# Attention in a two-layer transformer kernel: scores issued a head at a time, the product with the values in one block

## The chip, the cores and the metric

The kernel runs on one core of a Trainium2 chip. Its time is the device time of one execution in microseconds (us). TensorE, VectorE (DVE), ScalarE (ACT), GpSimd (POOL) and the DMA queue of SyncE (SP) each work through a list of instructions of their own, in order, and wait for each other by semaphores.

## The reference

Two layers over 2048 tokens of width 256, each `x + ga * attention(LN(x))` and then `x + gb * ffn(LN(x))`; shifts, scales and gates come from a small product. Attention has 16 heads of width 16. Cut to what matters here:

```python
# layer 0: causal, with a penalty that grows with the distance
S = jnp.einsum('hid,hjd->hij', K, Q) * HEAD_DIM ** -0.5
S = jnp.where(delta < 0, -jnp.inf, S) + decay          # decay = -(i - j)
C = jax.nn.softmax(S, axis=-1)
attn = jnp.einsum('hij,hjd->hid', C, V)
# layer 1: every token sees every token
scores = jnp.einsum('bhqd,bhkd->bhqk', q, k) * EMBED_DIM ** -0.5
probs = jax.nn.softmax(scores, axis=-1)
attn = jnp.einsum('bhqk,bhkd->bhqd', probs, v)
```

The softmax needs each row's maximum; the kernel computes the scores once to find the maxima and a second time, with the maximum already subtracted, for the exponentials.

## The kernel before

**Units and steps.** Attention goes by units: a unit is 512 rows (a chunk, of 4) times a group of four heads (of 4), 16 units a layer. A unit goes through its keys in steps of 128 keys: 16 steps a unit in layer 1, and 4, 8, 12 or 16 in layer 0 for chunks 0 to 3 (`steps_of`). So layer 0 has 160 steps and layer 1 has 256. In layer 0 the last four steps of each unit are diagonal: they leave out the first 0, 128, 256 or 384 rows (`off`) and add a triangle of -1e30 by two more products per head (line 690).

**One step.** For each of four heads: a score product (line 682), 128 keys by 512 rows, written to one of three PSUM banks (0, 1 and 2, in turn, over all steps); ScalarE's exponential (line 875) from that bank into `probs`, which has two buffers by step; and the product with the values (line 707) from `probs` into bank 7, where the unit's steps accumulate. The product with the values of step s is issued during step s + 1. A head's scores use 52 partitions that begin at 0 (even heads) or at 64 (odd heads). The four heads' values have 17 columns each and write to partitions 0, 32, 64 and 96 of bank 7; each float32 product is run as two instructions in the trace.

**Work beside the steps.** The maxima of a later unit are computed in pairs of heads: two score products (line 654, in layer 0 with the mask of line 660) into the two banks of a slot, and a reduction of 128 x 1024 by VectorE (line 1075). A reduction for each 128 rows, head pair and 512 keys makes 32 a unit in layer 1. There are two slots (banks 3 and 4, 5 and 6); nearly all other TensorE work that isn't a step (transposes, projections) takes a slot in turn too, and waits until the slot's work before last has been drained (`open_slot`). When all maxima of a unit are there, VectorE forms two parts of each (lines 1083 to 1088), TensorE transposes them (`mt`, line 667), ScalarE copies them and SP's DMAs place them among the rows (`place`). At a unit's end ScalarE copies bank 7 (`oc`, line 890), and TensorE transposes the sums (`ft`, line 717); after four units follow `bt`, `op`, `st`, `nm` and `ln`, the output projection and the next normalisation.

**What sets the order.** `attention_walk` writes one list by hand; every engine walks the same list and picks its own entries. For each step: the scores of heads 0 and 1 (`sc` with 0), the first half of the step's maxima, the first 256 columns of the last step's product with the values (`pv` with 0), the scores of heads 2 and 3 (`sc` with 1), the rest of the maxima, the other 256 columns (`pv` with 1), and then the transposes that fall to this step. At a unit's first step the whole 512 columns are in `pv` 0. Most steps have two pairs of maxima.

**Semaphores.** `s_e` counts completed scores, `s_p` exponentials, `s_pv` steps whose product is complete, `s_oc` copies of bank 7. A score e waits for exponential e - 3, the last user of its bank (counted from the kernel's first score); the product waits for all four exponentials of its step; a step's first exponential waits for the product of two steps before.

Of the kernel before, what the change touches and what calls it, by code (L numbers as in the profile page):

```python
# [10 lines left out]
ACT = mybir.ActivationFunctionType  # L11
AX = mybir.AxisListType

P = 128
# [4 lines left out]
CH = 512  # L19
# [64 lines left out]
def attention_walk(y, done):  # L84
# [15 lines left out]
    for n in range(NU):  # L100
        steps = steps_of(y, n)
        for k in range(steps):
# [5 lines left out]
            out += work[:half]  # L108
            if s:
                out.append(("pv", y, s - 1, m, j, 0))  # L110
            out.append(("sc", y, s, n, k, 1))
            out += work[half:]
            if s:
                out.append(("pv", y, s - 1, m, j, 1))
# [20 lines left out]
    out += [("pv", y, total - 1, NU - 1, steps_of(y, NU - 1) - 1, z) for z in range(2)] + [("oc", y, NU - 1)]  # L135
# [105 lines left out]
def adaln_two_layers(nc, a):  # L241
    ctx = ExitStack()
    with ctx:
# [343 lines left out]
        def _(pe):  # L587
# [83 lines left out]
            def scores(y, s, n, jt, hp):  # L671
                i, g = n // NG, n % NG
                if jt == 0 and hp == 0:
                    pe.wait_ge(s_mrow, 64 * (y * NU + n + 1))
                off = max(0, jt - TPC * i) * P if CAUSAL[y] else 0
                diag = CAUSAL[y] and jt >= TPC * i
                e = HG * (S0[y] + s) + 2 * hp
                for par in range(2):
                    if e + par >= 3:
                        pe.wait_ge(s_p, e + par - 2)  # L680
                    at = slice(64 * par, 64 * par + KS)
                    mm = pe.matmul(bank((e + par) % 3)[:, off:CH], keys[at, g * HP + hp, jt * P:(jt + 1) * P],  # L682
                                   rows[at, g, hp, off:CH], start=True, stop=not diag)
                    if not diag:
                        mm.then_inc(s_e, 1)
                if diag:
                    for z in range(2):
                        for par in range(2):
                            at = slice(64 * par, 64 * par + 64)
                            mm = pe.matmul(bank((e + par) % 3)[:, off:off + P], eye2[at, z, :], neg_e[at, z, :],  # L690
                                           start=False, stop=(z == 1))
                            if z == 1:
                                mm.then_inc(s_e, 1)

            def values(y, s, n, jt, z):
                i, g = n // NG, n % NG
                off = max(0, jt - TPC * i) * P if CAUSAL[y] else 0
                lo, hi = (max(off, z * CH // 2), (z + 1) * CH // 2) if jt else (0, CH * (1 - z))
                if z == 0:
                    pe.wait_ge(s_p, HG * (S0[y] + s + 1))  # L700
                if jt == 0 and z == 0:
# [3 lines left out]
                if lo < hi:  # L705
                    for h in range(HG):
                        mm = pe.matmul(psum[32 * h:32 * h + VW, 7, lo:hi], v_sb[:, jt, g * HG + h, :],  # L707
                                       probs[:, (S0[y] + s) % 2, h, lo:hi], start=(jt == 0),
                                       stop=(z == 1 and jt == steps_of(y, n) - 1))
                    if z == 1 or jt == 0:  # L710
                        mm.then_inc(s_pv, 1)
# [123 lines left out]
        def _(act):  # L835
# [29 lines left out]
            def exps(y, s, n, jt, hp):  # L865
                i = n // NG
                off = max(0, jt - TPC * i) * P if CAUSAL[y] else 0
                if s == 0 and y == 0 and hp == 0:
                    act.wait_ge(s_mod, NLAY)
                if S0[y] + s >= 2 and hp == 0:  # L870
                    act.wait_ge(s_pv, S0[y] + s - 1)
                for par in range(2):
                    e = HG * (S0[y] + s) + 2 * hp + par
                    act.wait_ge(s_e, e + 1)
# [371 lines left out]
```

## Time and profile before

| | |
|---|---|
| median of 3 runs | 1858.12 us (1856.98 to 1858.46) |
| profiled execution | 1858.49 us, span 1856.7 us |
| TensorE matmul, busy | 1653.7 us (89%), 12812 instructions |
| TensorE weight load, busy | 704.9 us (38%) |
| VectorE, busy | 1161.5 us (63%) |
| ScalarE, busy | 1005.3 us (54%) |
| GpSimd, busy | 61.4 us (3%) |
| maximum reductions, line 1075 | 832, 912.1 us |
| exponentials, line 875 | 1664, 845.7 us |
| product with the values, line 707 | 6144 instructions, 495.8 us |
| scores, line 682 | 1664, 352.0 us |

The profile is of one execution. Layer 0's attention runs from about 100 to 553 us, layer 1's from about 838 to 1485; the feed-forward stages lie between and behind them. Matmuls are pipelined, so a matmul's busy time (some 0.38 us for 512 columns) is longer than its distance to the next one; the distance from start to start is what adds up. In the windows below, each engine has its busy time and in brackets its count of instructions. In the rows in order of time, neighbouring instructions of one line are merged (x8), and the bracket at the end gives the idle time before the first and what released it.

### The profile page before, as it was taken

To read this page: it belongs to the slowest core of one execution; us is meant where nothing else is said; L and a number is where in the kernel's file an instruction comes from. 1 tells how busy PE (TensorE), PEld (TensorE's weight loads), DVE (VectorE), ACT (ScalarE), POOL (GpSimd) and SP (SyncE) were. 2 spreads that over 40 slices of the span, in tenths; PEclk is the share of its full clock that TensorE was granted. 3 is DMA by queue.
4 is the path that set the end of the run, shared out by engine and by line. 5 is a ranking of instruction groups with operands and counts; after the bars stand their busy time and mean duration, and the time that the engine had idled before them with its cause. 6 is when DMAs were issued, how large, how long until landed. Compare 5 with 4: busy or idle time off the path is not lost.

```text
span 1856.7 us, 32528 instructions
## 1 busy us (share of the span) xinstructions
PE 1653.7 (89%) x12812; PEld 704.9 (38%) x12812; DVE 1161.5 (63%) x1430; ACT 1005.3 (54%) x1913; POOL 61.4 (3%) x96
## 2 busy tenths in 40 slices
PE   7888989889999987758998999899999988999998
PEld 4533333333335543412333333333332243645545
DVE  4477887988802334494998999899899033121221
ACT  1145667768881111008997899789888913121110
POOL 1200000010000000300000000000000020000000
PEclk9879999999999999758999999999999989999999
DMA  7610000000000210110200000000000010000000
GB/s 204 137 53 11 12 9 6 11 6 2 2 1 29 58 40 20 41 19 5 84 6 6 6 6 10 2 11 6 6 2 2 1 40 0 10 3 12 1 12 12
DMA packets 39542, 41.87 MB, mean 23 GB/s; under 512 B 7172, under 2 KB 37828, under 8 KB 39388
## 3 DMA queue, kind: packets, MB, share of 16 engines
q1 hardware_dynamic: 39396, 39.79, 8.2%
q8 instruction: 108, 1.77, 0.4%
q14 instruction: 38, 0.31, 0.1%
HBM read 29.02 MB, written 10.49 MB: 21 GB/s over the span
## 4 chain that ended last, share of the span: by engine, by line
PE 32%; DVE 24%; ACT 3%; issue 2%; DVEq 0%; ACTq 0%
DVE mpart L1075 20%; PE psum L748 6%; PE psum L773 6%; PE psum L707 6%; PE psum L752 6%; PE psum L682 3%; ACT probs L875 3%; PE psum L654 2%; PE psum L627 1%; DVE probs L1103 1%; DVE key_region L1106 1%; PE psum L736 1%; PE psum L783 1%; PE psum L639 0%; DVE attn_region L1023 0%
## 5 line engine op out<-in xcount | busy, mean ns | idle before, releaser
L1075 DVE TENSOR_REDUCE mpart<-psum 128x2 f32<-128x1024 f32 (+2 forms) x832 | 912.1, 1158 | 103.8 <-PE psum L654 84.2
L875 ACT ACTIVATE probs<-psum 128x512 f32<-128x512 f32 (+3 forms) x1664 | 845.7, 573 | 188.1 <-PE psum L682 107.5
L707 PE MATMUL psum<-probs,v_region 128*17 128x256 f32 (+2 forms) x6144 | 495.8, 395 | 14.6 <-ACT out_sb L890 7.9
L654 PE MATMUL psum<-key_region,row_region 50*128 50x512 f16 (+3 forms) x1664 | 327.1, 385 | 94.3 <-DVE mpart L1075 79.8
L682 PE MATMUL psum<-row_region,key_region 52*128 52x512 f16 (+3 forms) x1664 | 352.0, 380 | 11.6 <-ACT probs L875 10.3
L682 PEld LDWEIGHTS psum<-row_region,key_region 52*128 52x128 f16 x1664 | 97.2, 93 | 367.3 <-ACT probs L875 286.5
L748 PE MATMUL psum<-hT,ffn_w 128*128 128x512 f32 (+1 forms) x320 | 162.2, 631 | 41.9 <-DVE key_region L1106 20.6
L707 PEld LDWEIGHTS psum<-probs,v_region 128*17 128x17 f32 x6144 | 102.8, 95 | 206.7 <-issue 101.5
L654 PEld LDWEIGHTS psum<-key_region,row_region 50*128 50x128 f16 x1664 | 94.7, 94 | 191.7 <-DVE mpart L1075 137.4
L752 PE MATMUL psum<-hT,ffn_w 128*128 128x512 f32 (+1 forms) x320 | 152.7, 600 | 0.0
L914 ACT ACTIVATE probs<-psum 128x512 f32<-128x512 f32 (+1 forms) x56 | 33.4, 597 | 199.4 <-PE psum L748 199.4
L1066 DVE TENSOR_TENSOR x_sb<-psum,x_sb 128x1024 f32<-128x1024 f32 x16 | 19.6, 1224 | 162.9 <-PE psum L773 137.4
L1103 DVE TENSOR_TENSOR probs<-psum,probs 128x512 f32<-128x512 f32 x44 | 30.4, 692 | 130.4 <-PE psum L752 130.4
L748 PEld LDWEIGHTS psum<-hT,ffn_w 128*128 128x128 f32 (+1 forms) x320 | 57.6, 192 | 114.1 <-issue 56.6
L773 PE MATMUL psum<-v_region,key_region 128*128 128x256 f32 x448 | 97.5, 379 | 1.7 <-DVE key_region L1106 1.7
L752 PEld LDWEIGHTS psum<-hT,ffn_w 128*128 128x128 f32 (+1 forms) x320 | 61.1, 191 | 81.3 <-issue 81.3
L773 PEld LDWEIGHTS psum<-v_region,key_region 128*128 128x128 f32 x448 | 85.0, 190 | 15.4 <-issue 3.9
L914 ACT ACTIVATE probs<-psum,gate_s 128x512 f32<-128x512 f32 (+1 forms) x24 | 16.5, 686 | 121.7 <-PE psum L748 121.7
L1099 DVE SCALAR_TENSOR_TENSOR key_region<-psum,up_s,probs 128x512 f32<-128x512 f32 (+1 forms) x24 | 18.0, 749 | 92.6 <-PE psum L752 68.4
L851 ACT ACTIVATE hT<-psum,modc 128x512 f32<-128x512 f32 x32 | 23.1, 775 | 79.4 <-PE psum L616 79.4
L924 ACT ACTIVATE probs<-psum 128x1024 f32<-128x1024 f32 (+1 forms) x24 | 22.8, 952 | 61.3 <-PE psum L761 61.3
L1109 DVE TENSOR_TENSOR key_region<-psum,probs 128x512 f32<-128x512 f32 (+1 forms) x12 | 8.3, 689 | 70.9 <-PE psum L752 70.9
(101 smaller groups left out, 920.6 us busy)
## 6 DMA issues: line engine op xcount, KB each, us to landing
parts<-key_region SPq DMA_DIRECT2D x32, 256.0 KB, 2.5
key_region<-parts SPq DMA_DIRECT2D x48, 128.0 KB, 4.4
row_region<-parts SPq DMA_DIRECT2D x192, 32.0 KB
key_region<-in_wmod SPq DMA_DIRECT2D x2, 1536.0 KB, 12.2
x_sb<-in_x SPq DMA_DIRECT2D x4, 512.0 KB, 8.4
row_region<-mrow_t SPq DMA_DIRECT2D x128, 2.0 KB
out<-x_sb SPq DMA_DIRECT2D x16, 128.0 KB, 1.8
ffn_w<-in_w_gate SPq DMA_DIRECT2D x1, 1760.0 KB, 8.4
```

The lines of the kernel that those rows point to most:

```text
L654: mm = pe.matmul(bank(b + par)[:, 0:w], rows[at, g, hp, r * P:(r + 1) * P], keys[at, g * HP + hp, q * CH:q * CH + w], start=True, stop=not ...
L682: mm = pe.matmul(bank((e + par) % 3)[:, off:CH], keys[at, g * HP + hp, jt * P:(jt + 1) * P], rows[at, g, hp, off:CH], start=True, stop=not ...
L707: mm = pe.matmul(psum[32 * h:32 * h + VW, 7, lo:hi], v_sb[:, jt, g * HG + h, :], probs[:, (S0[y] + s) % 2, h, lo:hi], start=(jt == 0), sto ...
L748: mm = pe.matmul(psum[0:f, b, :], up_gate[y][0][:, d, c * P:c * P + f], hT[:, d, tok], start=(d == 0), stop=(d == KD - 1))
L752: mm = pe.matmul(psum[0:f, b + 1, :], up_gate[y][1][:, d, c * P:c * P + f], hT[:, d, tok], start=(d == 0), stop=(d == KD - 1))
L773: mm = pe.matmul(both(b)[:, r * D:(r + 1) * D], hid[y][tc % 2][0:f, c, r * P:(r + 1) * P], down[y][0:f, c, :], start=(c == 0), stop=(c == ...
L851: ins = nc.scalar.activation(hT[:, c, tc * CH:(tc + 1) * CH], bank(b + c), ACT.Identity, bias=modc[:, y, i:i + 1], scale=modc[:, y, i + 2: ...
L875: nc.scalar.activation(probs[:, (S0[y] + s) % 2, 2 * hp + par, off:CH], psum[:, e % 3, off:CH], ACT.Exp, scale=SCALES[y]).then_inc(s_p, 1)
L914: nc.scalar.activation(sil[k % 2][0:f, :], psum[0:f, bank_of(item), :], ACT.Silu, scale=gate_s[0:f, c:c + 1] if y == 0 else 1.0).then_inc( ...
L924: nc.scalar.activation(wx[k % 2][:, 0:n, :], psum[:, bank_of(item):bank_of(item) + n, :], ACT.Identity).then_inc(drained(*item)[0], 1)
L1075: V.tensor_reduce(mpart[:, n % NG, at:at + 2, q:q + 1], psum[:, b:b + 2, 0:w], AX.X, ALU.max).then_inc(drained(*item)[0], 1)
L1103: V.tensor_tensor(utmp[k % 2], up, sil[k % 2], ALU.mult).then_inc(s_ut, 1)
```

## The change

`attention_walk` now issues, for each step: the score of head 0, the first half of the maxima, the scores of heads 1 and 2, the rest of the maxima, the score of head 3, and then the last step's product with the values over all its columns at once. `scores` and `exps` handle one head a call instead of two; in the diagonal steps a head's mask products follow its own score. `values` issues four products (eight instructions in the trace) of up to 512 columns instead of twice that many of 256. Banks, buffers and what each semaphore counts stay.

```diff
--- before.py
+++ after.py
@@ -106,12 +106,11 @@
             m, j = (n, k - 1) if k else (n - 1, steps_of(y, n - 1) - 1 if n else 0)
             out.append(("sc", y, s, n, k, 0))
             out += work[:half]
+            out += [("sc", y, s, n, k, h) for h in (1, 2)]
+            out += work[half:]
+            out.append(("sc", y, s, n, k, 3))
             if s:
-                out.append(("pv", y, s - 1, m, j, 0))
-            out.append(("sc", y, s, n, k, 1))
-            out += work[half:]
-            if s:
-                out.append(("pv", y, s - 1, m, j, 1))
+                out.append(("pv", y, s - 1, m, j))
             if s and k == 0:
                 out.append(("oc", y, n - 1))
             if k == 0 and n and n + 3 < NU:
@@ -132,7 +131,7 @@
                     out.append(("nm", 2 * y + 1, i))
                 if k == 6:
                     out.append(("ln", 2 * y + 1, i))
-    out += [("pv", y, total - 1, NU - 1, steps_of(y, NU - 1) - 1, z) for z in range(2)] + [("oc", y, NU - 1)]
+    out += [("pv", y, total - 1, NU - 1, steps_of(y, NU - 1) - 1), ("oc", y, NU - 1)]
     return out
 
 
@@ -668,47 +667,36 @@
                                    identh[:, :], start=True, stop=True)
                 mm.then_inc(filled(*item)[0], 1)
 
-            def scores(y, s, n, jt, hp):
+            def scores(y, s, n, jt, h):
                 i, g = n // NG, n % NG
-                if jt == 0 and hp == 0:
+                if jt == 0 and h == 0:
                     pe.wait_ge(s_mrow, 64 * (y * NU + n + 1))
                 off = max(0, jt - TPC * i) * P if CAUSAL[y] else 0
                 diag = CAUSAL[y] and jt >= TPC * i
-                e = HG * (S0[y] + s) + 2 * hp
-                for par in range(2):
-                    if e + par >= 3:
-                        pe.wait_ge(s_p, e + par - 2)
-                    at = slice(64 * par, 64 * par + KS)
-                    mm = pe.matmul(bank((e + par) % 3)[:, off:CH], keys[at, g * HP + hp, jt * P:(jt + 1) * P],
-                                   rows[at, g, hp, off:CH], start=True, stop=not diag)
-                    if not diag:
-                        mm.then_inc(s_e, 1)
+                e = HG * (S0[y] + s) + h
+                if e >= 3:
+                    pe.wait_ge(s_p, e - 2)
+                at = slice(64 * (h % 2), 64 * (h % 2) + KS)
+                mm = pe.matmul(bank(e % 3)[:, off:CH], keys[at, g * HP + h // 2, jt * P:(jt + 1) * P],
+                               rows[at, g, h // 2, off:CH], start=True, stop=not diag)
                 if diag:
+                    at = slice(64 * (h % 2), 64 * (h % 2) + 64)
                     for z in range(2):
-                        for par in range(2):
-                            at = slice(64 * par, 64 * par + 64)
-                            mm = pe.matmul(bank((e + par) % 3)[:, off:off + P], eye2[at, z, :], neg_e[at, z, :],
-                                           start=False, stop=(z == 1))
-                            if z == 1:
-                                mm.then_inc(s_e, 1)
-
-            def values(y, s, n, jt, z):
+                        mm = pe.matmul(bank(e % 3)[:, off:off + P], eye2[at, z, :], neg_e[at, z, :], start=False, stop=(z == 1))
+                mm.then_inc(s_e, 1)
+
+            def values(y, s, n, jt):
                 i, g = n // NG, n % NG
-                off = max(0, jt - TPC * i) * P if CAUSAL[y] else 0
-                lo, hi = (max(off, z * CH // 2), (z + 1) * CH // 2) if jt else (0, CH * (1 - z))
-                if z == 0:
-                    pe.wait_ge(s_p, HG * (S0[y] + s + 1))
-                if jt == 0 and z == 0:
+                pe.wait_ge(s_p, HG * (S0[y] + s + 1))
+                if jt == 0:
                     pe.wait_ge(*drained("v", y, (NCH - 1) if not CAUSAL[y] else i))
                     if y * NU + n:
                         pe.wait_ge(s_oc, y * NU + n)
-                if lo < hi:
-                    for h in range(HG):
-                        mm = pe.matmul(psum[32 * h:32 * h + VW, 7, lo:hi], v_sb[:, jt, g * HG + h, :],
-                                       probs[:, (S0[y] + s) % 2, h, lo:hi], start=(jt == 0),
-                                       stop=(z == 1 and jt == steps_of(y, n) - 1))
-                    if z == 1 or jt == 0:
-                        mm.then_inc(s_pv, 1)
+                off = max(0, jt - TPC * i) * P if CAUSAL[y] else 0
+                for h in range(HG):
+                    mm = pe.matmul(psum[32 * h:32 * h + VW, 7, off:CH], v_sb[:, jt, g * HG + h, :],
+                                   probs[:, (S0[y] + s) % 2, h, off:CH], start=(jt == 0), stop=(jt == steps_of(y, n) - 1))
+                mm.then_inc(s_pv, 1)
 
             def sums_transpose(item):
                 b = open_slot(item)
@@ -862,18 +850,17 @@
                     nc.scalar.activation(stage[(k - 1) % 2][:, f, 0, :], bank(bank_of(item) + f), ACT.Identity,
                                          bias=(b_row, b_col)[side][:, f:f + 1]).then_inc(s_h, 1)
 
-            def exps(y, s, n, jt, hp):
+            def exps(y, s, n, jt, h):
                 i = n // NG
                 off = max(0, jt - TPC * i) * P if CAUSAL[y] else 0
-                if s == 0 and y == 0 and hp == 0:
+                if s == 0 and y == 0 and h == 0:
                     act.wait_ge(s_mod, NLAY)
-                if S0[y] + s >= 2 and hp == 0:
+                if S0[y] + s >= 2 and h == 0:
                     act.wait_ge(s_pv, S0[y] + s - 1)
-                for par in range(2):
-                    e = HG * (S0[y] + s) + 2 * hp + par
-                    act.wait_ge(s_e, e + 1)
-                    nc.scalar.activation(probs[:, (S0[y] + s) % 2, 2 * hp + par, off:CH], psum[:, e % 3, off:CH],
-                                         ACT.Exp, scale=SCALES[y]).then_inc(s_p, 1)
+                e = HG * (S0[y] + s) + h
+                act.wait_ge(s_e, e + 1)
+                nc.scalar.activation(probs[:, (S0[y] + s) % 2, h, off:CH], psum[:, e % 3, off:CH],
+                                     ACT.Exp, scale=SCALES[y]).then_inc(s_p, 1)
 
             def copy_maximum(item):
                 act.wait_ge(*filled(*item))
```

## Rows read from the trace of the kernel before

**Rows 1.** Windows: layer 1 and its end; busy (count) of PE, PEld, DVE, ACT, POOL; clock, DMA

```profile
870.00:1440.00 570.00, 536.28 (x5410) 177.63 (x5402) 531.63 (x548) 490.30 (x924) 3.79 (x6) 0.99 0.04 12
1440.00:1485.00 45.00, 42.38 (x412) 11.65 (x409) 0.68 (x2) 43.50 (x85) 0.00 (x0) 1.00 0.01 1
```

**Rows 2.** Chain of waits, layer 1: start, length, engine, tile, line, count

```profile
1086.37 15.94 DVE mpart L1075 x14
...
1108.09 13.68 DVE mpart L1075 x12
1125.30 15.94 DVE mpart L1075 x14
```

**Rows 3.** Order in time (start, length), TensorE, a plain step

```profile
921.40 0.39 PE L682 MATMUL psum<-row_region,key_region 52*128 52x512 f16 x2
921.63 0.38 PE L654 MATMUL psum<-key_region,row_region 50*128 50x512 f16 x2
921.94 0.63 PE L707 MATMUL psum<-probs,v_region 128*17 128x256 f32 x8
922.50 0.42 PE L682 MATMUL psum<-row_region,key_region 52*128 52x512 f16 x2
...
923.63 0.39 PE L682 MATMUL psum<-row_region,key_region 52*128 52x512 f16 x2
```

**Rows 4.** Order in time, TensorE, a step without maxima

```profile
1446.47 0.58 PE L682 MATMUL psum<-row_region,key_region 52*128 52x512 f16 x2
1447.15 0.63 PE L707 MATMUL psum<-probs,v_region 128*17 128x256 f32 x8
1447.71 0.39 PE L682 MATMUL psum<-row_region,key_region 52*128 52x512 f16 x2
```

**Rows 5.** Order in time, TensorE, a unit's second step

```profile
955.53 1.05 PE L707 MATMUL psum<-probs,v_region 128*17 128x512 f32 x8 [0.40 <-ACT out_sb L890]
956.52 0.39 PE L682 MATMUL psum<-row_region,key_region 52*128 52x512 f16 x2
...
957.64 0.39 PE L682 MATMUL psum<-row_region,key_region 52*128 52x512 f16 x2
958.45 0.39 PE L654 MATMUL psum<-key_region,row_region 50*128 50x512 f16 x2 [0.42 <-DVE mpart L1075]
```

**Rows 6.** Order in time, lone scores, two places

```profile
1019.65 1.08 ACT L875 ACTIVATE probs<-psum 128x512 f32<-128x512 f32 x2
...
1020.30 0.39 PE L682 MATMUL psum<-row_region,key_region 52*128 52x512 f16 x1 [0.69 <-ACT probs L875]
...
1020.51 0.40 PE L654 MATMUL psum<-key_region,row_region 50*128 50x512 f16 x2
...
1441.44 0.09 PEld L682 LDWEIGHTS psum<-row_region,key_region 52*128 52x128 f16 x1 [0.33 <-ACT probs L875]
...
1441.76 0.41 PE L707 MATMUL psum<-probs,v_region 128*17 128x256 f32 x4
```

**Rows 7.** Order in time, from a score to its exponential

```profile
942.20 0.39 PE L682 MATMUL psum<-row_region,key_region 52*128 52x512 f16 x2
...
942.62 1.75 ACT L875 ACTIVATE probs<-psum 128x512 f32<-128x512 f32 x3 [0.42 <-PE psum L682]
...
1006.84 0.39 PE L682 MATMUL psum<-row_region,key_region 52*128 52x512 f16 x2
...
1007.32 1.63 ACT L875 ACTIVATE probs<-psum 128x512 f32<-128x512 f32 x3 [3.81 <-PE psum L682]
```

**Rows 8.** Order in time, TensorE, behind the transposed maxima

```profile
940.52 0.39 PE L682 MATMUL psum<-row_region,key_region 52*128 52x512 f16 x2
...
941.32 0.39 PE L654 MATMUL psum<-key_region,row_region 50*128 50x512 f16 x2 [0.41 <-DVE mpart L1075]
```

**Rows 9.** Order in time, TensorE, a diagonal step

```profile
472.02 0.30 PE L690 MATMUL psum<-neg_e,eye 64*128 64x128 bf16 x4
472.13 0.40 PE L654 MATMUL psum<-key_region,row_region 50*128 50x512 f16 x2
```

## The prediction

> **What bounds the kernel now.** Two attention stages, 160 steps in the causal layer 0 and 256 in layer 1, take more than half of the time. I read the windows by stretch first [rows 1]. From 870 to 1440 us TensorE, VectorE and ScalarE are all 86 to 94% busy, so no share tells which one sets the pace; the reader is to see only that TensorE's clock is full (0.99) and that the last 45 us have hardly any VectorE work and ScalarE busy for 43.5. Then the chain of waits: in layer 1 its long pieces are maximum reductions, a unit of 16 steps begins again every 38.93 us (1125.30 - 1086.37), and from x14 against x12 one reduction costs (15.94 - 13.68) / 2 = 1.13 us [rows 2]. Two reductions a step are 2.26 us, 32 a unit 36.2 us. Then the order in time of a plain step [rows 3]: pair of scores, pair of maxima (+0.23), half of the product with the values (+0.31), next pair of scores (+0.56), and the same again: 921.40 to 923.63 is 2.23 us. VectorE falls behind by 0.03 a step and is caught up where the walk puts transposes. So the stage is tied: VectorE 2.26, TensorE's own instructions 2 x (0.23 + 0.31 + 0.56) = 2.2, ScalarE four exponentials. In steps without maxima the pace is 2.12 us [rows 4], and there the circle is visible: second score pair at 1446.47, its exponentials, values at 1447.15 (+0.68), next scores at 1447.71 (+0.56).
>
> **The change, part by part.** Nothing is computed differently; SP's and POOL's lists keep their order, and the transfers' waits count the same completed scores. Three things change on TensorE.
>
> *Half as many instructions with the values.* Two times (0.31 + 0.56) per step becomes one block of eight 512-column instructions. Such a block exists at each unit's first step: 955.53 to the next score 956.52, 0.99 us [rows 5]. Entry stays as it is after a lone score, 0.32 (1441.44 to 1441.76) [rows 6]. So 1.74 becomes 1.31 and the gain is 0.43 minus what follows.
>
> *Pairs of scores broken.* Heads of a pair lie in partitions 0 and 64 and both stream in the same 0.23 us [rows 3]. Now head 0 stands alone before a maximum, heads 1 and 2 pair up, head 3 stands alone: three slots of 0.23 for scores where there were two. A lone score is followed by the next maxima after 0.21 (1020.30 to 1020.51) [rows 6], so it does cost a slot and hides nothing. TensorE's own time per step is then 4 x 0.23 (head 0, maxima, heads 1 and 2, maxima) + 0.32 (head 3) + 0.99 = 2.23 against 2.2 before: nothing gained or lost. Bounds of a lone score: 0 (if the next maximum could stream beside it) and 0.23; I take 0.21 to 0.23, since the row shows it, and it will turn out not to matter, for the next term is longer.
>
> The Trainium skill (TensorEngine Tiling (Array Packing), Key Properties) says that changing the tiling mode drains TensorE. Scores take half the rows and the values' product a quarter of the columns, so the change halves the changes of mode, and the rows agree that they cost: 0.32 into the product against 0.23 between scores and maxima, and 0.13 lost per block (2 x 0.56 - 0.99). By that rule alone the step gets shorter by 0.2 us; its page TensorE: Matmul & The Clock Gate (Part 3) says that it is matmuls in distinct row groups that run at once, which takes the same 0.2 back for the broken pair. Were the rule on modes alone at work, the time would be that of rival 1.
>
> *A new wait, and this one decides.* Scores rotate through three banks: score e waits for exponential e - 3. For head 3 that is head 0 of the same step. Before, head 3 came 1.1 us after head 0 and the half product stood between two such circles; now head 3 is directly ahead of the whole product in TensorE's queue, and behind it wait the product, the next head 0 and the next maxima. The circle is head 0 -> exponential -> head 3 -> product -> next head 0. Its terms: score to exponential 0.48 with ScalarE idle (1006.84 to 1007.32; for the second half's first exponential it is 0.42, 942.20 to 942.62, so head 0 pays 0.06 more) [rows 7]; from the exponential's start to the score that waited for its bank 1020.30 - 1019.65 = 0.65 [rows 6]. So head 3 starts 0.48 + 0.65 = 1.13 after head 0, though its turn comes at 4 x 0.23 = 0.92. Then 0.32 and 0.99. Sum 1.13 + 0.32 + 0.99 = **2.44 us a step**, whether or not there are maxima. The same terms give today's 2.12: second score pair, 0.42, one exponential ahead in ScalarE's queue 0.49 (at most 43.5 us / 85 = 0.51), 0.65, together 1.56, + 0.56 = 2.12 [rows 1, 4, 6, 7]. ScalarE (4 x 0.5) and VectorE (2.26) both fit in 2.44, so they idle; a second maximum waits for its slot until 0.70, within 0.02 of its turn, and head 3's wait covers it.
>
> *The steps that are long today get shorter,* since VectorE no longer lags. In a regular unit of layer 1 38.93 - 16 x 2.23 = 3.25 us lie over the plain pace. Today the copy of the sums leaves TensorE idle for 0.40 ahead of the product, the transpose of the sums adds 0.56 (956.52 to 957.64 is 1.12, a half step's 0.56 without it), and the maximum behind it waits 0.58 for a slot (957.64 to 958.45 where 0.23 is usual) [rows 5]; the rest is around the transposed maxima, where I take 0.33 for the transpose itself, four products that fill one bank and stream in about a score's 0.23 with its turn-round, and a slot wait follows (940.52 to 941.32, 0.80 for 0.23) [rows 8]. After: the copy of the sums is out of TensorE's way but ahead of head 0's exponential, +0.12; the sums' transpose +0.6; its slot wait under head 3's; transposed maxima +0.33 and their slot wait +0.1 and +0.34 (VectorE has two reductions and the three small operations on the maxima, for which I take 0.8, still queued). Sum 1.5. So a regular unit changes by 16 x 0.21 - (3.25 - 1.5) = 3.3 - 1.75 = +1.6 us.
>
> **The sum.** Layer 1, units 1 to 13: 13 x 1.6 = +21 (three contain the output projection, whose stretch is VectorE's chain and absorbs a little; unit 1 has spare time before and loses more; they cancel). Units 0, 14 and 15: 32 steps without maxima x (2.44 - 2.12) = +10, and few plain ones: +11. Layer 0: by the walk 22 steps have no maxima, 14 of them full, 14 x 0.32 = 4.5; of the 82 other full ones I take half at the plain pace, 41 x 0.21 = 8.5 (the rest, with three or four maxima or beside transposes, wait for VectorE); its 64 diagonal steps lose the packing of the mask products too (the masks of two heads take 0.11 a half step, 472.02 to 472.13 [rows 9]; now each head has its own, some 0.2 to 0.4 more in the first two of four, less in the last two whose products are short), and many of them wait for three or four reductions a step anyway: +3. Together +16. Total 21 + 11 + 16 = +48. The profiled execution took 1858.5 (span 1856.7, 1.8 around it), 0.4 above the median of the runs, 1858.1; 1858.1 + 48 = **1906 us**.
>
> **The rivals.**
> 1. *VectorE stays the bound, faster* (7%). If head 0's exponential were done by 0.92 the circle would be TensorE's own 2.23 and the step VectorE's 2.26; a unit would be 36.2 + about 1.9 for the two other jobs of VectorE = 38.1, -0.8 x 14 = -11, steps without maxima +0.11 x 40 = +4: 1851. It decides from a way from head 0 to head 3 below 0.97 (2.26 + 0.02 - 0.32 - 0.99); the rows say 1.13. For it: today's plain step waits on TensorE for little, and half the mode changes go.
> 2. *The long waits hide it, slower by less* (17%). If stretches of layer 0 and the boundaries of units are VectorE's or POOL's chains more than I think, only layer 1's plain steps pay: about 130 x 0.21 less the boundary gain, and the steps without maxima: +20 to +30, 1883.
> 3. *The two streams beat against each other* (11%). Product, next head 0 and next maximum now come in one lump: 1.77 us without a new maximum (0.23 + 0.32 + 0.99 + 0.23). Where VectorE has one narrow causal reduction queued it starves, and after each transpose a late maximum delays head 3, then the whole product. At 0.3 more for each of the 64 diagonal steps and a unit's boundary: +15 to +20, 1924.
> 4. *No change* (4%): rivals 1 and the lone scores cancel.
> My forecast, 1890 to 1918, has 61%. The range 1876 to 1926 reaches into rivals 2 and 3 and leaves out rival 1 and their ends. About 0.2% (3.7 us) is what a measurement of this kernel can tell from no change: faster 0.07, same 0.04, slower 0.89.
>
> **What would show it.** Right: plain steps of layer 1 at 2.44 us, with and without maxima alike; head 3 alone, 1.13 after head 0, its weight load ended by ScalarE's exponential; VectorE waiting for TensorE some 0.15 a step instead of the reverse; eight 512-column instructions taking 0.99 to the next score; a unit at 40.5. Wrong: head 3 at 0.92 and steps at 2.26 (rival 1); steps at 2.44 but units still at 39 (rival 2); layer 0 losing more than 25 us (rival 3). The forecast falls if the exponential of a lone head 0 begins sooner than 0.48 or if a block of eight leaves sooner than 0.99 when it accumulates, for the block that I read is a unit's first.

## The result and the profile after

The change makes the kernel slower. The median of four runs is 1929.1 us (1914.0 to 1942.3) against 1857.9 us (1857.0 to 1858.5) for the kernel before: a ratio of 1.038, 95% interval 1.030 to 1.046. The direction was forecast; the size was not: 1906 was predicted, and 1929 lies 3 us above the upper end of the range. The profiled execution took 1942.3 us with a span of 1940.5; it is the slowest of the four, 13 us above their median. The four runs spread over 28 us, those of the kernel before over 1.5; nine later runs of the kernel before, though, went from 1855.6 to 1866.2.

The page, its rows of busy time and of TensorE's clock in 40 slices of 48.5 us (tenths of full speed):

```profile
PE 1719.5 (89%) x9996; PEld 663.8 (34%) x9996; DVE 1176.9 (61%) x1430; ACT 993.1 (51%) x1913; POOL 63.7 (3%) x96
PEclk9888989989959998755999999999999989999999
```

ScalarE's and VectorE's work is what it was (busy within 1.4%), and TensorE has 2,816 instructions fewer, which is the halved product with the values. In the clock the reader is to see the lone 5 in the twelfth slice (534 to 582 us). Of the groups, the product with the values and the weight loads of the scores:

```profile
L697 PE MATMUL psum<-probs,v_region 128*17 128x512 f32 (+3 forms) x3328 | 444.9, 609 | 0.1
L680 PEld LDWEIGHTS psum<-row_region,key_region 52*128 52x128 f16 x1664 | 127.6, 96 | 496.4 <-ACT probs L862 421.9
```

The weight loads of the scores (line 680) now sit 422 us behind ScalarE's exponentials, where it was 287 in the kernel before. A plain step of layer 1, TensorE's instructions in order of time, the place that answers to [rows 3]:

```profile
985.88 0.39 PE L680 MATMUL psum<-row_region,key_region 52*128 52x512 f16 x1
985.89 0.60 PE L653 MATMUL psum<-key_region,row_region 50*128 50x512 f16 x2
986.12 0.59 PE L680 MATMUL psum<-row_region,key_region 52*128 52x512 f16 x2
986.51 0.41 PE L653 MATMUL psum<-key_region,row_region 50*128 50x512 f16 x2
987.02 0.39 PE L680 MATMUL psum<-row_region,key_region 52*128 52x512 f16 x1
987.34 1.05 PE L697 MATMUL psum<-probs,v_region 128*17 128x512 f32 x8
988.32 0.39 PE L680 MATMUL psum<-row_region,key_region 52*128 52x512 f16 x1
```

Head 3 comes 1.14 after head 0 (987.02 - 985.88), the product 0.32 later, the next head 0 0.98 later: 2.44 us, the circle of the prediction term by term. The same line of the scores in the last layer-0 unit, where there are no maxima, with ScalarE's exponentials:

```profile
545.60 1.03 PE L680 MATMUL psum<-row_region,key_region 52*128 52x512 f16 x3
546.30 2.06 ACT L862 ACTIVATE probs<-psum 128x512 f32<-128x512 f32 x4 [1.66 <-PE psum L680]
546.96 0.60 PE L680 MATMUL psum<-row_region,key_region 52*128 52x512 f16 x1 [0.32 <-ACT probs L862]
547.49 1.91 PE L697 MATMUL psum<-probs,v_region 128*17 128x512 f32 x8
549.33 0.61 PE L680 MATMUL psum<-row_region,key_region 52*128 52x512 f16 x2
```

545.60 to 549.33 is 3.73 us. The circle is the same, but each of TensorE's parts in it is longer: head 0 to its exponential 0.70 instead of 0.48, into the product 0.53 instead of 0.32, the product 1.84 instead of 0.98; only the exponential to head 3 is as before, 0.66 against 0.65. The windows say why (busy us and count of PE, PEld, DVE, ACT and POOL, then the clock):

```profile
530.00:533.20 3.20, 2.35 (x24) 0.73 (x24) 0.00 (x0) 2.17 (x7) 0.00 (x0) 1.00 0.01 3
533.20:583.00 49.80, 45.98 (x176) 7.11 (x175) 0.68 (x2) 27.44 (x55) 0.00 (x0) 0.50 0.00 1
...
880.00:915.00 35.00, 30.58 (x109) 4.04 (x109) 3.09 (x6) 20.35 (x39) 0.00 (x0) 0.50 0.00 1
...
932.00:1490.00 558.00, 523.03 (x3532) 132.91 (x3525) 513.56 (x519) 453.26 (x869) 3.80 (x6) 1.00 0.04 12
...
1530.00:1567.00 37.00, 28.86 (x188) 6.54 (x184) 0.68 (x2) 31.17 (x62) 0.00 (x0) 1.00 0.00 1
```

Two of the three stretches without maxima run at 1.2 GHz, the third, with the very same steps, at 2.4. They did not come to it alike. The first stretch was entered at 2.4 GHz, behind a layer-0 unit's short diagonal steps, and the clock fell 2.3 us after its first score, at 533.2. The second began at 1.2 GHz, as it does in every kernel here, and stayed there for 38 us, until the maxima began again. A step of the third stretch:

```profile
1538.21 0.60 PE L680 MATMUL psum<-row_region,key_region 52*128 52x512 f16 x3
1539.35 0.39 PE L680 MATMUL psum<-row_region,key_region 52*128 52x512 f16 x1 [0.53 <-ACT probs L862]
1539.66 1.05 PE L697 MATMUL psum<-probs,v_region 128*17 128x512 f32 x8
1540.65 0.60 PE L680 MATMUL psum<-row_region,key_region 52*128 52x512 f16 x3
```

That is 2.44 us, of which TensorE is idle for 0.53. In the kernel before the first stretch had 0.95 (3.4 us at 1.2 GHz, then full again) and the second came back within its first 12 us:

```profile
517.40:553.40 36.00, 33.31 (x344) 10.33 (x340) 0.68 (x2) 31.45 (x65) 0.00 (x0) 0.95 0.00 1
838.00:850.00 12.00, 9.79 (x64) 2.17 (x60) 2.53 (x5) 9.88 (x18) 0.00 (x0) 0.72 0.00 1
850.00:875.00 25.00, 24.40 (x256) 7.29 (x255) 11.92 (x11) 24.11 (x47) 0.00 (x0) 1.00 0.01 1
```

Where the 83.8 us between the two spans lie, from the start of the first score of each unit in both traces:

| stretch | before | after | difference |
|---|---|---|---|
| up to the first step | 99.5 | 94.0 | -5.5 |
| layer 0, units 0 to 14 | 417.9 | 436.9 | +19.0 |
| layer 0, unit 15, 15 of its steps, no maxima | 34.1 | 55.6 | +21.5 |
| its last step and the feed-forward stage | 286.6 | 294.1 | +7.6 |
| layer 1, unit 0, mostly without maxima | 37.5 | 52.1 | +14.7 |
| layer 1, units 1 to 13 | 537.6 | 557.2 | +19.6 |
| layer 1, units 14 and 15 (31 steps) | 70.4 | 77.5 | +7.1 |

The rows add up to 84.0; the last 373 us are alike in both to 0.1, and the rest is rounding. The first row is no part of the change: over the nine traces of this case the first score lies between 94.0 and 99.8 us, and in a second trace of the changed kernel at 99.3.

### The profile page after: what moved, and what is told of

It is laid out like the page before. It is cut to its first block, busy times and chain, and to the rows that moved or that the text cites. A ratio compares the mean times of both kernels' runs of the same rounds, so it can differ in the third digit from the quotient of the medians.

```text
span 1940.5 us, 26865 instructions
## 1 busy us (share of the span) xinstructions
PE 1719.5 (89%) x9996; PEld 663.8 (34%) x9996; DVE 1176.9 (61%) x1430; ACT 993.1 (51%) x1913; POOL 63.7 (3%) x96
## 4 chain that ended last, share of the span: by engine, by line
PE 41%; DVE 13%; ACT 6%; issue 2%; ACTq 0%; DVEq 0%
PE psum L697 11%; DVE mpart L1062 8%; PE psum L680 7%; PE psum L736 6%; PE psum L761 6%; PE psum L740 5%; ACT probs L862 5%; PE psum L653 2%; PE psum L626 1%; DVE probs L1090 1%; DVE key_region L1093 1%; PE psum L724 1%; PE psum L638 1%; PE psum L771 0%; PE psum L705 0%
## 5 line engine op out<-in xcount | busy, mean ns | idle before, releaser
L1062 DVE TENSOR_REDUCE mpart<-psum 128x2 f32<-128x1024 f32 (+2 forms) x832 | 923.7, 1159 | 124.9 <-PE psum L653 99.7
L862 ACT ACTIVATE probs<-psum 128x512 f32<-128x512 f32 (+3 forms) x1664 | 831.8, 578 | 277.7 <-PE psum L680 193.3
L680 PE MATMUL psum<-row_region,key_region 52*128 52x512 f16 (+3 forms) x1664 | 504.8, 390 | 44.2 <-ACT probs L862 27.8
L653 PE MATMUL psum<-key_region,row_region 50*128 50x512 f16 (+3 forms) x1664 | 407.8, 392 | 95.9 <-DVE mpart L1062 67.9
L697 PE MATMUL psum<-probs,v_region 128*17 128x512 f32 (+3 forms) x3328 | 444.9, 609 | 0.1
L680 PEld LDWEIGHTS psum<-row_region,key_region 52*128 52x128 f16 x1664 | 127.6, 96 | 496.4 <-ACT probs L862 421.9
L1053 DVE TENSOR_TENSOR x_sb<-psum,x_sb 128x1024 f32<-128x1024 f32 x16 | 19.6, 1225 | 167.3 <-PE psum L761 137.4
L697 PEld LDWEIGHTS psum<-probs,v_region 128*17 128x17 f32 x3328 | 56.1, 96 | 101.8 <-issue 74.4
L685 PE MATMUL psum<-neg_e,eye 64*128 64x128 bf16 x512 | 65.1, 229 | 0.0
L839 ACT ACTIVATE hT<-psum,modc 128x512 f32<-128x512 f32 x32 | 23.2, 775 | 77.5 <-PE psum L615 77.5
```

The source lines that it names most:

```text
L653: mm = pe.matmul(bank(b + par)[:, 0:w], rows[at, g, hp, r * P:(r + 1) * P], keys[at, g * HP + hp, q * CH:q * CH + w], start=True, stop=not ...
L680: mm = pe.matmul(bank(e % 3)[:, off:CH], keys[at, g * HP + h // 2, jt * P:(jt + 1) * P], rows[at, g, h // 2, off:CH], start=True, stop=not ...
L685: mm = pe.matmul(bank(e % 3)[:, off:off + P], eye2[at, z, :], neg_e[at, z, :], start=False, stop=(z == 1))
L697: mm = pe.matmul(psum[32 * h:32 * h + VW, 7, off:CH], v_sb[:, jt, g * HG + h, :], probs[:, (S0[y] + s) % 2, h, off:CH], start=(jt == 0), s ...
L839: ins = nc.scalar.activation(hT[:, c, tc * CH:(tc + 1) * CH], bank(b + c), ACT.Identity, bias=modc[:, y, i:i + 1], scale=modc[:, y, i + 2: ...
L862: nc.scalar.activation(probs[:, (S0[y] + s) % 2, h, off:CH], psum[:, e % 3, off:CH], ACT.Exp, scale=SCALES[y]).then_inc(s_p, 1)
```

## The experiments

**Only the block: pairs of scores kept.** The first question is whether the circle or TensorE's own work sets 2.44 us. The two give opposite signs for this order:

```diff
-            out.append(("sc", y, s, n, k, 0))
+            out += [("sc", y, s, n, k, h) for h in (0, 1)]
             out += work[:half]
-            out += [("sc", y, s, n, k, h) for h in (1, 2)]
+            out += [("sc", y, s, n, k, h) for h in (2, 3)]
             out += work[half:]
-            out.append(("sc", y, s, n, k, 3))
```

> Only one part of the change: pairs of scores kept (heads 0 and 1, first maxima, heads 2 and 3, rest of the maxima), product with the values in one block at the step's end. Circle theory (head 3 waits for head 0's exponential and stands ahead of the block): head 0 to head 3 1.13, the second maxima 0.21, into the block 0.31, block 0.99 = 2.65 us a plain step with maxima, 2.44 without; the kernel as a whole slower than the changed one by about 0.2 us in each of some 250 steps, near 1960 to 1990. Rival, TensorE's own instructions: 3 x 0.23 + 0.32 + 0.99 = 2.0, so VectorE's 2.26 sets the step, and the kernel is near 1850.

Measured: 1993.6 us, 1.070 times the kernel before (1.065 to 1.075), just over the 1960 to 1990 expected. A plain step of layer 1:

```profile
1180.84 0.39 PE L679 MATMUL psum<-row_region,key_region 52*128 52x512 f16 x2
1181.06 0.38 PE L652 MATMUL psum<-key_region,row_region 50*128 50x512 f16 x2
1181.28 0.38 PE L679 MATMUL psum<-row_region,key_region 52*128 52x512 f16 x1
1181.97 0.39 PE L679 MATMUL psum<-row_region,key_region 52*128 52x512 f16 x1 [0.31 <-ACT probs L861]
1182.18 0.40 PE L652 MATMUL psum<-key_region,row_region 50*128 50x512 f16 x2
1182.51 1.05 PE L696 MATMUL psum<-probs,v_region 128*17 128x512 f32 x8
1183.49 0.39 PE L679 MATMUL psum<-row_region,key_region 52*128 52x512 f16 x2
```

2.65 us, as the circle says. Head 3 is torn off its pair and starts 1.13 after head 0; now the second maxima stand behind it too. Of the two halves of the change, the block at the step's end is what costs; taking the heads one at a time repairs 0.21 us of it, because head 3's wait is then spent on the maxima. This kernel loses clock too: ten steps of layer 0's last unit and ten of layer 1's first take 3.73 us.

**Only the heads: the product in two halves.**

```diff
             out.append(("sc", y, s, n, k, 0))
             out += work[:half]
+            if s:
+                out.append(("pv", y, s - 1, m, j, 0))
             out += [("sc", y, s, n, k, h) for h in (1, 2)]
             out += work[half:]
             out.append(("sc", y, s, n, k, 3))
             if s:
-                out.append(("pv", y, s - 1, m, j))
+                out.append(("pv", y, s - 1, m, j, 1))
 ...
```

> Only the other part: scores a head at a time as in the change, but the product in two halves, the first behind the first maxima, the second behind head 3. Own instructions of TensorE: 0.23 + 0.31 + 0.56 + 0.23 + 0.23 + 0.32 + 0.56 = 2.44 a step with maxima. Circle theory: heads 1 to 3 are scored late and their three exponentials must end before the next first half: 0.42 + 2 x 0.49 + 0.65 = 2.05 after heads 1 and 2, + 0.56 = 2.61 us a step, with and without maxima. If a lone head costs nothing and no circle binds: 2.26. Whole kernel near 1950 by the circle, near 1900 by the instructions.

Measured: 1981.0 us, 1.063 (1.057 to 1.070). In the steps, from heads 1 and 2 on:

```profile
1156.57 0.39 PE L682 MATMUL psum<-row_region,key_region 52*128 52x512 f16 x2
...
1157.32 0.63 PE L702 MATMUL psum<-probs,v_region 128*17 128x256 f32 x8
1157.88 0.39 PE L682 MATMUL psum<-row_region,key_region 52*128 52x512 f16 x1
...
1158.62 0.63 PE L702 MATMUL psum<-probs,v_region 128*17 128x256 f32 x8
1159.18 0.39 PE L682 MATMUL psum<-row_region,key_region 52*128 52x512 f16 x2
```

Heads 1 and 2 to the next first half 2.05 us (three exponentials in a row), + 0.56 = 2.61, with and without maxima alike. The circle is right to 0.01 in another place; here it goes through the wait of the product, not through a bank. The whole is 31 us over the 1950 expected: this kernel too ran its steps at 1.2 GHz for a while in each layer (3.47 us without maxima), which the expectation left out. In layer 1's last unit the clock fell in the middle of equal steps, which had run at 2.4 GHz and 2.61 us until then:

```profile
1553.00:1579.00 26.00, 20.07 (x188) 4.75 (x185) 0.68 (x2) 20.39 (x40) 0.00 (x0) 1.00 0.00 1
1580.00:1606.00 26.00, 26.00 (x155) 3.99 (x151) 0.00 (x0) 16.00 (x30) 0.00 (x0) 0.50 0.00 1
```

So each part of the change alone is worse than both together, and TensorE's own work sets neither.

**The circle shortened at ScalarE.**

```diff
-                nc.scalar.activation(probs[:, (S0[y] + s) % 2, h, off:CH], psum[:, e % 3, off:CH],
+                end = min(CH, off + CH // 2) if h == 0 else CH
+                nc.scalar.activation(probs[:, (S0[y] + s) % 2, h, off:end], psum[:, e % 3, off:end],
 ...
```

> The changed kernel, but the exponential of head 0 of each step covers 256 columns instead of 512 (the other half of head 0's probabilities is left as it was, so that part of the computation is left out). Circle theory: the exponential takes 0.38 instead of 0.60, head 3 comes 0.91 after head 0, the circle 2.23, and the step falls from 2.44 to about 2.26 (VectorE) with maxima and 2.23 without. Rival (the lone heads' and the block's own time, or PSUM traffic, set 2.44): the step stays at 2.44. Whole kernel about 50 us below the changed one.

Measured: 1871.5 us, ratio to the kernel before 1.008 (1.004 to 1.012), 58 us below the changed kernel's 1929. Seven of the eight runs lie between 1867.7 and 1872.6, one at 1895.8. A step without maxima (TensorE's matmuls and ScalarE):

```profile
1466.39 0.39 PE L680 MATMUL psum<-row_region,key_region 52*128 52x512 f16 x1 [0.32 <-ACT probs L863]
...
1466.70 1.05 PE L697 MATMUL psum<-probs,v_region 128*17 128x512 f32 x8
...
1467.69 0.60 PE L680 MATMUL psum<-row_region,key_region 52*128 52x512 f16 x3
1468.17 1.36 ACT L863 ACTIVATE probs<-psum 128x256 f32<-128x256 f32 x3 [0.37 <-PE psum L680]
1468.61 0.39 PE L680 MATMUL psum<-row_region,key_region 52*128 52x512 f16 x1 [0.32 <-ACT probs L863]
```

Head 3 to head 3 is 2.22 us, and head 3 comes 0.92 after head 0 (1468.61 - 1467.69) where it was 1.14; steps with maxima alternate between 2.26 and 2.33, VectorE's pace and a little more. Nothing but head 0's exponential was changed on the path, and 0.22 us a step is gone: the exponential of head 0 lies in the circle. The rival (own work of TensorE) is out. The 58 us of the whole kernel are not the circle alone: in layer 0's last unit this kernel kept 2.4 GHz, and 15 of its steps took 34.4 us against 55.6, where 0.22 a step make 3. In layer 1's first unit it had 1.2 GHz as the changed kernel, ten steps of 3.51.

**The changed kernel again.**

> The changed kernel again, for its clock. Its times spread over 28 us while those of the kernel before spread over 1.5. Theory: the spread is TensorE's clock in the stretches without maxima, where a step is 2.44 us at 2.4 GHz and 3.73 at 1.2. Then the steps with maxima are 2.44 again to 0.01, and the time differs from 1942 by the length of the 1.2 GHz spans around 530 to 590 and 840 to 920 us alone, 1.29 us for each step in them. Rival: the spread lies in the plain steps too.

Measured: 1946.6 us in the profiled execution and 1936.4 in the other, with 1860.2 for the kernel before beside them. Steps with maxima are 2.44 again, and the 1.2 GHz spans have the same lengths as in the first trace (58 and 82 us); the two profiled executions are 4.3 us apart, 5.3 later at the first score (94.0 against 99.3 us) and 1.4 less in layer 0. So this trace doesn't show the spread, and the expectation that the low spans alone set the time did not come true for this pair. What is left is the mean clock that each execution reports: 0.926 with 1942.3 us and 0.947 with 1914.0. That is 2 x (1 - 0.926) x 1940.5 = 287 us at 1.2 GHz against 203. 84 us fewer, if all of them lay in steps that take 3.73 there and 2.44 otherwise, are 84 x 1.29 / 3.73 = 29 us; measured 28.4. For the two other executions (0.942 and 0.938) the same sum gives 22 and 17 us, and measured are 16.3 and 10.1. So the clock goes with the time, but that it makes the whole spread is not shown; where in the faster execution it came back wasn't recorded.

**Steps without maxima in the old order, the rest changed.** Only the 54 steps without maxima differ from the changed kernel, the last 22 of layer 0 and the first 10 and last 22 of layer 1:

```diff
+            if work:
                 ...
+            else:
+                out += [("sc", y, s, n, k, h) for h in (0, 1)]
+                if s:
+                    out.append(("pv", y, s - 1, m, j, 0))
+                out += [("sc", y, s, n, k, h) for h in (2, 3)]
+                if s:
+                    out.append(("pv", y, s - 1, m, j, 1))
 ...
```

> The changed kernel, but the 54 steps without maxima keep the order of the kernel before (two heads, half a product, two heads, half a product). Clock theory: in the changed order these steps leave TensorE idle so much that its clock, once it is at 1.2 GHz, stays there (3.73 us a step); in the old order they are 2.12 and the clock comes back within some 7 us. So no 1.2 GHz span of over 20 us at 530 or at 880 us, steps without maxima 2.12, and what is left over the kernel before is the circle in the steps with maxima, +1.6 a unit in layer 1 and some 12 to 18 in layer 0: 1885 to 1900. Rival (the clock falls for another reason, such as the longer steps before the stretch): the spans stay and the time is over 1920.

Measured: 1889.0 us (1887.3 to 1902.6), 1.020 (1.016 to 1.023), 40 us below the changed kernel's 1929.1 (the kernel before measured 1855.4 beside this run and 1857.9 beside that one). Windows of the same two stretches:

```profile
523.00:556.00 33.00, 30.58 (x295) 8.82 (x293) 0.68 (x2) 29.14 (x59) 0.00 (x0) 0.95 0.01 2
...
847.00:858.00 11.00, 9.14 (x44) 1.67 (x42) 2.72 (x5) 7.97 (x14) 0.00 (x0) 0.50 0.01 1
858.00:887.00 29.00, 27.65 (x234) 6.95 (x232) 13.02 (x11) 26.45 (x52) 0.00 (x0) 1.00 0.01 1
```

The clock is back in both; only the first 11 us of layer 1 are at 1.2 GHz, a stretch that begins so in every kernel here.

**The reverse: the kernel before, with the changed order in those 54 steps alone.** The condition above turned round. One thing of the change stays in the other steps: in the diagonal ones a head's mask products follow its own score.

> The kernel before, but the 54 steps without maxima take the changed order (four heads, then the product in one block). Circle theory at full clock: 0.32 more in each of about 46 of them, +15: 1873. Clock theory: the stretch from 530 us on and the one that begins layer 1 run at 1.2 GHz, 3.73 us a step for some 21 steps, +27 more and a few us in the stage that follows: 1900 to 1908, with a spread of 10 us or more between runs; the steps with maxima stay at 2.23.

Measured: 1900.7 us, 1.024 (1.022 to 1.025), so 45 us for 54 of 416 steps:

```profile
515.00:565.00 50.00, 45.05 (x188) 7.29 (x188) 0.68 (x2) 28.30 (x56) 0.00 (x0) 0.56 0.00 1
...
857.00:895.00 38.00, 33.42 (x120) 4.43 (x122) 2.92 (x6) 22.32 (x42) 0.00 (x0) 0.50 0.01 1
```

Both stretches are at 1.2 GHz again, 3.73 us a step (the first fell to it at 520, 5 us after its first score, from a clock of 1.00), while the units around them run as in the kernel before (38.9 us). The spread of 10 us or more didn't come: 1895.0 to 1901.7.

**More work, faster.** The changed kernel with two scores issued twice in 53 of the 54 steps without maxima (not in layer 0's last):

```diff
 ...
+                if h in (1, 2) and (y, s) in idle_steps:
+                    pe.matmul(bank(e % 3)[:, off:CH], keys[at, g * HP + h // 2, jt * P:(jt + 1) * P],
+                              rows[at, g, h // 2, off:CH], start=True, stop=True)
 ...
```

> The changed kernel, but in the 54 steps without maxima the scores of heads 1 and 2 are issued twice into the same banks (the second overwrites the first with the same numbers). TensorE's list ahead of head 3 grows to 4 x 0.23 = 0.92, still below the 1.13 at which head 0's exponential lets head 3 go, so at full clock the step stays 2.44 us although more is computed. Clock theory: the added work keeps or brings back 2.4 GHz, so the stretches at 530 and 880 us take 2.44 a step instead of 3.73 and the kernel gets faster by doing more: near 1905. Rival (the work between the waits doesn't matter): 3.73 as before or longer, 1940.

Measured: 1902.9 us (1897.0 to 1911.9), 1.027 (1.024 to 1.030), 26 us below the changed kernel although it computes 106 scores more. A step of the last layer-0 unit (line 689 is the added score) and the two windows:

```profile
536.08 0.39 PE L691 MATMUL psum<-row_region,key_region 52*128 52x512 f16 x1
536.09 0.60 PE L689 MATMUL psum<-row_region,key_region 52*128 52x512 f16 x2
536.31 0.59 PE L691 MATMUL psum<-row_region,key_region 52*128 52x512 f16 x2
537.22 0.39 PE L691 MATMUL psum<-row_region,key_region 52*128 52x512 f16 x1 [0.32 <-ACT probs L873]
537.53 1.05 PE L708 MATMUL psum<-probs,v_region 128*17 128x512 f32 x8
538.52 0.39 PE L691 MATMUL psum<-row_region,key_region 52*128 52x512 f16 x1
```

```profile
523.00:560.00 37.00, 32.25 (x242) 9.06 (x238) 0.68 (x2) 30.12 (x61) 0.00 (x0) 1.00 0.00 1
...
858.00:887.00 29.00, 26.63 (x178) 6.04 (x174) 13.02 (x11) 24.30 (x48) 0.00 (x0) 0.98 0.01 1
```

The step is 2.44 us, as at full clock it must be, since the added scores fit ahead of head 3's wait. Layer 1's first unit has four steps at 3.74 and then 2.44. The circle is untouched, and more work at an unchanged circle can't itself save time: what moved is the clock. From the first score on, the two profiled executions (the changed kernel's slowest run, this one's fastest) are 47 us apart: 18 in layer 0's last unit, 12 in its last step and the feed-forward stage, 8 in layer 1's first unit, nothing behind it, and 10 in units 0 to 13 of layer 0. In those last the two kernels have the same instructions, so there the clock gave other times to equal work. This kernel is 47.5 us slower than the kernel before (1902.9 - 1855.4, run beside it). It is the changed kernel without most of its loss of clock, near the +48 of the prediction; that the two agree to 0.5 us is luck, since its runs lie 15 us apart and its first 16 us of layer 1 are still at 1.2 GHz.

## Why the prediction was wrong, point by point

**What bounds the kernel: right.** Neither TensorE's work nor VectorE's reductions but a circle through ScalarE. It gave 2.44, 2.65, 2.61 and 2.23 us for four kernels, and measured were 2.44, 2.65, 2.61 and 2.22. The shorter exponential moved it as the circle says, and neither half of the change follows TensorE's own work.

**Half as many instructions with the values: right.** A block leaves after 0.98 also when it accumulates.

**Pairs of scores broken: wrong, without effect on the step.** A lone head was charged a slot of its own, from one row [rows 6]. In the trace after, the first maxima start 0.01 after the lone head 0 (985.89 against 985.88), and heads 1 and 2 0.23 after that. TensorE's own work in a step is thus less than the 2.23 that the prediction had; four slots of 0.22 for scores and maxima, the way into the product and the block make 0.88 + 0.10 + 0.98 = 1.96. The row of before was misread: there the maxima's weight load came only 0.18 after the score's (1020.48 against 1020.29), and between them the trace has two pieces in which TensorE passes semaphore waits, from 1020.29 and 1020.40. That these, and not an array that was taken, held it up is read from the trace and not tested. The 0.27 that 1.96 is below 2.23 never showed in a step, because the circle is longer. As the prediction said, head 3's wait covers this term.

**The long steps get shorter: right.** Forecast for a regular unit 38.93 + 1.6 = 40.5 us, measured 40.48 in units 2, 3, 6, 7, 10 and 11. Units 1 to 13 gave +19.6 for +21. The terms lie where they were put: the second step is 3.16, 0.72 over 2.44 (forecast 0.12 + 0.6), and the two steps around the transposed maxima are 0.42 and 0.32 over it (forecast 0.77 together).

**The step that failed is in the sum: "2.44 us a step, whether or not there are maxima", with TensorE's clock taken as full throughout.** The prediction had the clock at 0.99 for the stretch from 870 to 1440 us, and its check on steps without maxima came from the last stretch, at full clock too. It did not ask what 0.53 us of idle TensorE in each step of 2.44 would do to a clock that in the kernel before already fell for a moment in the first stretch (at 520 us) and was low at the start of the second. At 1.2 GHz the circle is 3.73. That is 1.29 us in each of some 21 steps, 27 us, and a few more in the feed-forward stage, which begins at 1.2 GHz and has it until 591 us. Layer 0's last unit came to +21.5 where about +4 was in the sum; layer 1's unit 0, with the units 14 and 15, to +21.8 where +11 was. In the profiled execution the sum missed by 36 us: 17.5 in layer 0's last unit, 10.8 in these units of layer 1, 7.6 in the feed-forward stage and 7 in the rest of layer 0, less 5.5 ahead of the first score and 1.4 in layer 1's other units. The two experiments that take most of the clock loss away agree: 1902.9 us (more work) and 1889.0 us (old order in these steps, which also takes back the 0.32 us of each). What makes the clock fall in one stretch and not in another of the same steps stays open.

**Layer 0, units 0 to 14: +19.0 for about +12.** About 10 us of it are clock again: second steps of three units (7, 8 and 11) are 1.5 to 2.1 us longer than before and lie in short spans at 1.2 GHz that the kernel before doesn't have there. The kernels with more work and with the old order in the steps without maxima have the changed kernel's instructions in units 0 to 13 and show it: these units take 387.9 and 386.9 us there, 397.8 in the changed kernel and 381.1 before. Unit 11 keeps its span in both.

**The rivals.** Rival 1 (VectorE stays the bound) asked for head 3 less than 0.97 after head 0; it comes 1.14 after it, and the kernel with the block alone refutes it too. Rival 2 (long waits hide it) holds nowhere in layer 1: even the units with an output projection take 50.7 us where two of them took 49.4 and one 50.3. Rival 3 named a mechanism for a time over 1920, and by its sign, layer 0 losing more than 25 us, it came out: layer 0 lost 40. But with the clock mostly back (more work) it lost 12, so the sign was met by another cause. The clock, which set the miss, was no rival at all.

None of these kernels beats the kernel before. Its order puts two scores, one half product, two scores, one half product, each half 1.1 us long, which is about the time that a bank needs to come free (1.13); each order tried here that gives that balance up is slower. That the balance is the reason is a reading; no run changes it alone.

## What to carry to other kernels

Where PSUM banks rotate through two engines, write down the circle from a bank's write to its next write, and see which long instruction stands behind the waiting one in the queue: moving a block can cost its whole wait even when it makes TensorE's own work shorter. Check each order at both of TensorE's clocks: a loop in which TensorE waits for another engine in every step ran at either one here, and then the same steps have two prices (2.44 and 3.73). The spread of the runs is a weak hint at that: the kernel with more work spread over 15 us, the reverse kernel, with its long spans at 1.2 GHz, over 7. The clock in windows of the trace shows it, and a few redundant matmuls in the gap tell it apart in one run.

## What the runs showed of the hardware

**The same steps ran at either level of the clock.** A step without maxima ran at 2.4 GHz for 37 us (1530 to 1567, TensorE busy 28.9 of 37) and at 1.2 GHz for 50 and for 35 us (busy 46.0 of 49.8 and 30.6 of 35), in one execution. The level isn't simply kept from the start: the first of these stretches was entered at 2.4 GHz and fell after 2.3 us, and in the kernel with heads alone the clock fell after 26 us and more of equal steps at 2.4. Once low in the changed order it stayed low until other work came. In the old order the clock came back 7 us (kernel before) and 11 us (old order in these steps only) after layer 1's first score, with the doubled scores after some 16 us, and with heads alone after 7. The Trainium skill (TensorE: Matmul & The Clock Gate, Part 1) describes a clock that is released by sustained activity; the trace agrees that busier steps bring it back (after 16 us with the doubled scores), and shows that the steps of this change do not (35 us and more at 1.2 GHz).

**Matmuls of different row groups overtake each other.** In the changed order the maxima of the odd head, listed behind those of the even head, start beside the lone even score, 0.01 after it, while the even head's maxima follow in the next slot. Their common semaphore comes only when both are done: the trace has it at 986.51, though the instruction that carries it had started at 985.89. So a lone half-height product costs no slot here, where a neighbour in the list uses the other half.
